# A two-layer model's routing rounds, spread over 128 partitions and summed by TensorE

## The reference

```python
def coor_descent(s, k):                     # s: 8 x 512 scores, EPS = 1
    logk = jnp.log(k)                       # k = 256 * 9/8 = 288
    def body(_, ab):
        a, b = ab
        a = EPS * (logk - logsumexp((s + b) / EPS, axis=-1, keepdims=True))
        b = -relu(s + a)
        return (a, b)
    a, b = fori_loop(0, 50, body, (zeros, -s))
    return exp((s + a + b) / EPS)
sel_scores, sel_idx = top_k(scores, 256)
```

## Time and profile before

| | |
|---|---|
| median of 3 runs | 1802.65 us (1799.55 to 1802.8) |
| the profiled execution | 1800.32 us, span of its instructions 1798.6 us |
| mean granted TensorE clock | 0.973 |
| PE / DVE / ACT / POOL busy, share of the span | 91% / 83% / 74% / 75% |
| layer 1 | 571.6 to 1798.6 us |

### The profile page before, as it was taken

One profiled execution on the slowest core, in us unless ns is written; L12 is line 12 of the kernel. 1 busy time (PEld: TensorE's weight loads), 2 busy tenths in 40 slices (PEclk: granted clock), 3 DMA queues, 4 the chain that ended last, 5 costly groups with the idle time before them and its releaser, 6 DMA issues.

```text
span 1798.6 us, 44374 instructions
## 1 busy us (share of the span) xinstructions
PE 1635.7 (91%) x13580; PEld 1007.8 (56%) x13580; DVE 1496.9 (83%) x2798; ACT 1334.3 (74%) x3261; POOL 1354.5 (75%) x1114
## 2 busy tenths in 40 slices
PE   6999899899884868799999999999999989999988
PEld 4676686685662444455456456456546445645645
DVE  6837848668465999989989989989989988988997
ACT  4756657666652777968978988887896897797765
POOL 2807807718644068999899999899998999989995
PEclk9989999999996989999999999999999999999999
DMA  9446445645466644465364546347345446355430
GB/s 279 147 127 144 132 136 142 167 152 120 142 167 167 171 132 108 126 158 136 115 169 118 143 135 153 114 119 175 114 129 133 104 137 176 95 143 154 110 94 25
DMA packets 164993, 247.65 MB, mean 138 GB/s; under 512 B 30776, under 2 KB 109304, under 8 KB 164760
## 3 DMA queue, kind: packets, MB, share of 16 engines
q1 hardware_dynamic: 152472, 228.02, 45.4%
q0 software_dynamic: 12288, 16.79, 4.6%
HBM read 168.08 MB, written 73.50 MB: 134 GB/s over the span
## 4 chain that ended last, share of the span: by engine, by line
PE 36%; DVE 14%; issue 8%; ACT 8%; POOL 1%; DMA 1%; DVEq 0%; SPq 0%; ACTq 0%; POOLq 0%
PE bank L2323 32%; DVE bank L2846 4%; DVE HB L2846 3%; PE bank L2423 3%; ACT bank L2636 2%; DVE HB L2851 2%; DVE SU L2818 1%; ACT PR L2674 1%; ACT PT L2558 1%; POOL HB L2274 1%; DVE nmax L2877 1%; PE bank L2451 1%; DVE rows L2793 1%; PE bank L2333 1%; DVE nmax L2874 0%
## 5 line engine op out<-in xcount | busy, mean ns | idle before, releaser
L2274 POOL TENSOR_TENSOR HB<-DD,BC 128x512 f32<-128x512 f32 x512 | 641.9, 1284 | 102.4 <-DMA DD<-SU 51.8
L2636 ACT ACTIVATE bank<-DD,A 128x512 f32<-128x512 f32 x512 | 350.3, 694 | 108.8 <-DVE HB L2851 68.7
L2280 POOL TENSOR_TENSOR HB<-HB,BC 128x512 f32<-128x512 f32 x256 | 323.1, 1277 | 49.2 <-DVE HB L2846 48.6
L2846 DVE TENSOR_TENSOR_SCAN bank<-bank,HB 128x512 f32<-128x512 f32 x256 | 311.1, 1215 | 25.8 <-ACT bank L2636 21.6
L2846 DVE TENSOR_TENSOR_SCAN HB<-bank,HB 128x512 f32<-128x512 f32 x256 | 310.3, 1212 | 15.7 <-ACT bank L2636 11.7
L2851 DVE TENSOR_TENSOR HB<-bank,BC 128x512 f32<-128x512 f32 x256 | 175.4, 685 | 15.3 <-DVE bank L2846 0.5
L692 POOL DMA_INDIRECT X<-expert_out_scratch,slot x64 | 110.8, 1731 | 63.9 <-DMA expert_out_scratch<-YS 38.1
L2323 PE MATMUL bank<-HB,fold 128*32 128x512 f32 x1024 | 136.8, 606 | 15.0 <-DVE HB L2851 7.1
L2423 PE MATMUL bank<-ident,PR 128*128 128x128 f32 x768 | 113.6, 279 | 18.1 <-ACT PR L2667 8.5
L2423 PEld LDWEIGHTS bank<-ident,PR 128*128 128x128 f32 x768 | 86.8, 141 | 76.3 <-issue 44.9
L2558 ACT ACTIVATE PT<-bank 128x512 f32<-128x512 f32 x192 | 109.1, 597 | 21.4 <-PE bank L2423 19.7
(11 more groups left out here) (287 smaller groups left out, 3591.9 us busy)
## 6 DMA issues: line engine op xcount, KB each, us to landing
DD<-dd_scratch SPq DMA_DIRECT2D x488, 128.0 KB, 3.5
ROW<-row_scratch SPq DMA_DIRECT2D x64, 256.0 KB
BC<-ssm_scratch SPq DMA_DIRECT2D x128, 128.0 KB, 4.1
dd_scratch<-SU SPq DMA_DIRECT2D x16, 1024.0 KB, 6.0
US<-us_scratch SPq DMA_DIRECT2D x32, 512.0 KB, 4.6
us_scratch<-SU SPq DMA_DIRECT2D x15, 1024.0 KB, 6.1
XL<-sorted_scratch SPq DMA_DIRECT2D x92, 128.0 KB, 2.4
expert_out_scratch<-YS SPq DMA_DIRECT2D x92, 128.0 KB, 1.8
```

The source lines that it names most:

```text
L2274: done(pool.tensor_tensor(HB[:, c % HR], du, bc, ALU.mult), "dbu")
L2280: done(pool.tensor_tensor(h, h, bc, ALU.mult), "cg")
L2636: done(act.activation(PD[n % 2][:], delta, ACT.Exp, scale=A[:, k:k + 1]), "dA")
L2846: done(dve.tensor_tensor_scan(h if n % 2 else dA, dA, h, 0.0, ALU.mult, ALU.add), "scan")
```

## The change

The rounds work on all 128 partitions. `spread_es` holds the 8 x 512 values as 128 x 32, 16 partitions to a batch; it has a second load from HBM and a second exponential. `part` is then a partial sum of 32 values on each partition. A new PE step `rs` after each of the 49 `rt` multiplies it with `blocks`, 128 x 128, which has ones where two partitions belong to one batch, so that every partition receives its batch's sum, in column 0 of bank `PY`. The next `rt` reads its limit there. The last sum is made for 8 partitions only. `blocks` lies in the memory of `YR` and is made by POOL in `constants`, three instructions more. `fold` of the first group waits also for `kr` and `keys`, which read the same bank.

```diff
-        es, rows, part = sb("es", [T]), sb("rows", [T]), sb("part", [2])
-        first, kinv = sb("first", [1]), sb("kinv", [1])
+        es, rows, part = sb("es", [T]), sb("rows", [T]), sb("part", [1])
+        first, kinv, spread_es, small = sb("first", [1]), sb("kinv", [1]), sb("spread_es", [T // 16]), sb("small", [T // 16])
+        blocks = YR[:, 0, 0:P]
...
-            ("s_in", [(es[0:B], scr["s"][:].rearrange("b p t -> b (p t)"))]),
+            ("s_in", [(spread_es[:], scr["s"][:].rearrange("b p t -> (b p t)").rearrange("(q j) -> q j", q=P)),
+                      (es[0:B], scr["s"][:].rearrange("b p t -> b (p t)"))]),
...
+                    own.now(pool.memset(blocks, 1.0))
+                    for base, step, channel in ((0, -16, 1), (15, 16, -1)):
+                        own.now(pool.affine_select(out=blocks.rearrange("p (g r) -> p g r", r=16),
+                                                   in_=blocks.rearrange("p (g r) -> p g r", r=16),
+                                                   compare_op=ALU.is_ge, fill=0.0, base=base,
+                                                   pattern=[[step, B], [0, 16]], channel_multiplier=channel))
...
+                def sum_blocks(i):
+                    after(pe, "rt", 0, i)
+                    if i == 0:
+                        pe.wait_ge(s["consts"], BLOCKS)
+                    if i < ROUTE_ITERS - 2:
+                        q = mm(PY[:, 0:1], blocks, part[:])
+                    else:
+                        q = mm(PY[0:B, 0:1], blocks.rearrange("p (g r) -> p g r", r=16)[:, :, 0], part[:])
+                    done(q, "rs")
...
                     if g == 0:
                         pe.wait_ge(s["consts"], CONSTS)
+                        after(pe, "kr", 0, 0)
+                        after(pe, "keys", 0, 0)
...
-                    act.wait_ge(over["s_in"], 16)
+                    act.wait_ge(over["s_in"], 32)
+                    act.activation(spread_es[:], spread_es[:], ACT.Exp)
                     done(act.activation(es[0:B], es[0:B], ACT.Exp), "es")
...
                 def limit(i):
                     if i:
-                        after(dve, "rt", 0, i - 1)
-                        return part[0:B, (i - 1) % 2:(i - 1) % 2 + 1]
+                        after(dve, "rs", 0, i - 1)
+                        return PY[:, 0:1]
...
                     r = limit(i)
-                    done(dve.scalar_tensor_tensor(out=rows[0:B], in0=es[0:B], scalar=r,
-                                                  in1=kinv[0:B].broadcast_to([B, T]), op0=ALU.min, op1=ALU.mult,
-                                                  accum_out=part[0:B, i % 2:i % 2 + 1]), "rt")
+                    done(dve.scalar_tensor_tensor(out=small[:], in0=spread_es[:], scalar=r,
+                                                  in1=kinv[:].broadcast_to([P, T // 16]), op0=ALU.min, op1=ALU.mult,
+                                                  accum_out=part[:]), "rt")
```

More of the change, by code:

```diff
@@ L1555 @@
[L1555 to L1560, removed]
[10 rows of a table removed]
-    "silu": [[67, 71, 69, 68], [513], [1097], [1760], [2360], [3014], [3651], [4274]],
@@ L1572 @@
[L1572 to L1579, removed]
@@ L1884 @@
[L1884 to L1888 removed]
+    "xt": [[0, 1], [391, 432], [951, 1012], [1643, 1645], [2288, 2291], [2899, 2900], [3528, 3531], [4125, 4122]],
@@ new lines @@
+    "xrt": [[50, 65], [671, 681], [1318, 1356], [1990, 2001], [2651, 2653], [3233, 3269], [3903, 3904], [4464,
+        4580]],
+    "xrtc": [[51, 66], [672, 682], [1319, 1364], [2002, 2003], [2652, 2656], [3234, 3270], [3905, 3906], [4465,
+        4581]],
+    "gam": [[64, 55, 54, 185, 184, 149]],
+    "proj": [[73, 136, 167, 158, 81, 145, 148, 182, 267, 174, 244, 315, 317, 388, 345, 343, 390, 444, 413, 428, 591,
[10 rows of a table added]
+    "silu": [[82, 87, 86, 83], [560], [1158], [1786], [2423], [3069], [3700], [4323]],
@@ new lines @@
+    "dtb": [[94]],
+    "abs": [[95, 96, 97, 98], [636, 612, 613, 656], [1220, 1214, 1215, 1265], [1882, 1863, 1881, 1895], [2517, 2507,
+        2515, 2518], [3160, 3139, 3156, 3161], [3801, 3782, 3783, 3816], [4410, 4401, 4441, 4411]],
+    "projc": [[104, 137, 168, 197, 193, 146, 194, 196, 268, 195, 254, 353, 357, 398, 356, 344, 399, 449, 414, 429,
[10 rows of a table added]
+    "us_st": [[105, 225], [562], [1175], [1862], [2506], [3128], [3778], [4324]],
+    "ssm": [[107], [561], [1168], [1803], [2424], [3089], [3710], [4366]],
@@ new lines @@
+    "relu": [[125, 126, 134, 135], [751, 750, 642, 704], [1269, 1250, 1231, 1232], [1977, 1848, 1845, 1847], [2637,
+        2636, 2477, 2478], [3272, 3271, 3120, 3127], [3932, 3931, 3813, 3814], [4526, 4483, 4435, 4436]],
+    "gsilu": [[128]],
+    "sln": [[144, 159], [703], [1323], [1950], [2576], [3211], [3886], [4511]],
+    "del": [[156, 279], [752, 705], [1367, 1324], [2020, 1951], [2638, 2577], [3277, 3219], [3933, 3887], [4548,
+        4525]],
+    "du": [[157, 339], [767, 766], [1408, 1377], [2031, 2000], [2678, 2578], [3278, 3221], [3934, 3910], [4566,
+        4565]],
@@ new lines @@
+    "dd_ld": [[160, 162, 164, 163, 203, 166, 400, 405, 534, 538, 539, 540, 655, 659, 661, 667], [824, 823, 850, 849,
[7 rows of a table added]
+    "dbu": [[161, 176, 183, 199, 175, 200, 305, 269, 329, 311, 310, 328, 365, 366, 392, 382, 389, 386, 406, 407,
[28 rows of a table added]
+    "asc": [[186]],
[29 rows of a table added]
+    "scan": [[190, 245, 248, 252, 287, 277, 306, 307, 354, 351, 360, 359, 375, 374, 403, 383, 418, 395, 425, 424,
[28 rows of a table added]
+    "score": [[201, 209, 259, 296, 441, 494, 554, 606, 650, 688, 714, 746], [829, 844, 982, 1039, 1155, 1233, 1244,
[5 rows of a table added]
+    "max": [[202, 205, 223, 226, 266, 260, 301, 316, 460, 442, 495, 496, 557, 563, 625, 607, 673, 651, 693, 689,
[10 rows of a table added]
@@ new lines @@
+    "turnc": [[264, 253, 289, 265, 303, 293, 415, 381, 486, 504, 572, 601, 618, 635, 668, 645, 732, 725, 726, 742,
[39 rows of a table added]
+    "recx": [[257, 304, 313, 347, 662, 779], [892, 901, 1100, 1195, 1348, 1440], [1560, 1589, 1660, 1711, 1963,
+        2051], [2147, 2228, 2312, 2467, 2605, 2704], [2826, 2902, 2942, 3048, 3228, 3326], [3432, 3525, 3590, 3667,
+        3867, 3988], [4104, 4192, 4265, 4393, 4533, 4578], [4697, 4791, 4923, 4932, 5077, 5165]],
+    "kr": [[258]],
+    "keys": [[262]],
+    "fold": [[276, 364, 385, 416, 452, 479, 544, 559, 602, 630, 654, 694, 744, 782, 835, 868], [908, 938, 976, 1017,
[7 rows of a table added]
@@ new lines @@
+    "kst": [[282]],
+    "value": [[284, 348, 371, 528, 617, 643, 683, 684, 762, 783, 785, 847], [965, 1019, 1146, 1218, 1292, 1327,
[5 rows of a table added]
+    "spread": [[290, 312, 346, 524, 690, 806], [893, 966, 1122, 1196, 1349, 1451], [1577, 1631, 1708, 1835, 1971,
+        2063], [2193, 2255, 2343, 2494, 2615, 2746], [2827, 2941, 3047, 3140, 3250, 3360], [3522, 3560, 3643, 3727,
+        3898, 4004], [4165, 4206, 4357, 4394, 4542, 4673], [4781, 4820, 4931, 4962, 5121, 5168]],
+    "spreadc": [[291, 314, 350, 527, 691, 807], [911, 968, 1128, 1222, 1354, 1466], [1584, 1657, 1709, 1836, 1976,
+        2064], [2197, 2263, 2345, 2495, 2621, 2747], [2891, 2945, 3051, 3155, 3257, 3391], [3524, 3561, 3644, 3747,
+        3899, 4010], [4182, 4207, 4358, 4404, 4543, 4688], [4785, 4851, 4963, 4979, 5123, 5175]],
@@ new lines @@
+    "norm": [[295, 349, 410, 529, 692, 848], [967, 1021, 1147, 1225, 1357, 1488], [1656, 1690, 1780, 1879, 1980,
+        2101], [2259, 2302, 2412, 2523, 2622, 2770], [2932, 2983, 3061, 3165, 3259, 3409], [3526, 3575, 3696, 3797,
+        3900, 4043], [4199, 4248, 4384, 4428, 4547, 4690], [4786, 4902, 4964, 5002, 5131, 5182]],
+    "widen": [[302, 367, 434, 553, 712, 881], [1011, 1054, 1160, 1262, 1370, 1509], [1669, 1697, 1795, 1914, 1985,
+        2123], [2290, 2315, 2413, 2533, 2642, 2788], [2949, 2984, 3063, 3177, 3275, 3421], [3537, 3579, 3704, 3811,
+        3927, 4044], [4247, 4267, 4427, 4456, 4560, 4705], [4845, 4921, 5001, 5033, 5132, 5183]],
@@ new lines @@
+    "ranks": [[338], [777], [1423], [2103], [2685], [3329], [3973], [4609]],
+    "dd_st": [[340], [788], [1409], [2032], [2681], [3279], [3955], [4574]],
+    "sel": [[363, 362, 341, 342], [818, 890, 891, 830], [1434, 1536, 1537, 1435], [2113, 2115, 2117, 2114], [2727,
+        2794, 2803, 2732], [3330, 3371, 3438, 3331], [3974, 3996, 4014, 3975], [4610, 4683, 4622, 4629]],
+    "xg": [[369], [910], [1554], [2202], [2868], [3480], [4063], [4796]],
+    "h_load": [[], [370], [936], [1558], [2238], [2876], [3481], [4102]],
@@ L1889 @@
+    "out": [[1023, 1006, 1022, 1016], [1611, 1605, 1603, 1602], [2272, 2260, 2258, 2195], [2978, 2977, 2976, 2975],
+        [3548, 3547, 3540, 3462], [4262, 4261, 4259, 4249], [4853, 4852, 4770, 4769], [5209, 5212, 5211, 5210]],
+    "tailp": [[], [], [], [], [], [], [], [5188, 5197, 5200, 5202]],
 }
@@ L2058, in layer1 @@
         ]
-        CONSTS = 9
+        CONSTS, BLOCKS = 9, 12
```

(2 more changed lines are left out.)

150 lines of the change are left out of this document (59 added, 91 removed), and 512 rows, old and new, of the table L1_ORDER.

## The result

The changed kernel took 1812.9 us (median of 10 runs, 1808.9 to 1818.3) against 1802.7 for the kernel before on the same chip: a ratio of 1.0057, interval 1.0041 to 1.0073. That is 10 us slower, where 6 were forecast. The profiled execution of the changed kernel took 1814.11 us.

What follows compares the result with a forecast made beforehand. It took DVE to bound layer 1's opening, with rounds a dependent chain. DVE lateness 5, toll 2 and clock 3.5, less 4.5 given back, made +6 us: 1806.3 profiled, 1808.5 us median, range 1791 to 1822.

Steps and rivals of the forecast that it cites:

- the trip: Layer 1's opening: one round from DVE to PE and back, put at 0.8 us, against 0.78 before.
- A first sum: PE's queue: the first sum of each of 22 groups finds its partial ready and costs about 0.25 us.
- the 27 whole trips: PE's queue in the opening: the other 27 sums each cost a whole 0.8 us, 21.6 us in all.
- the 3.6 us put ahead of them: Net extra DVE work before the keys: 5.9 us moved ahead, 2.3 left for later.
- the toll: Opening: rounds slowed beside POOL's products; 2 us taken, between 0.4 and 5.4.
- growth with length: Opening: if slowing beside POOL scales with a round's length, 0.06 us per round, 0.4 in all.
- the clock, +3.5: Opening, PE: one clock drop slows two projections to 3.45 us each, +3.5 us; bounds nothing to +31.
- Rival (d): PE's clock stays at 1.2 GHz through the rounds, +15 to +31 us on PE, 1820 to 1835; chance 0.10.
- so I give back 60% of DVE's: -4.5: From 670 to 760 us, DVE's 7.35 us idle gaps absorb 4.5 us of the 10.5 us lateness.
- I count 0 for it, with 4 us either way: Reordered table behind the opening: equal work up to each scan, so 0 us, with 4 either way.
- (b): DVE's freed time in the opening counts: 5 to 11 us faster, 1792 to 1798; chance 0.28.
- (c): Idle gaps absorb the opening's lateness: within 0.2%, 1799 to 1806 us; chance 0.20.

Runs made afterwards that it cites:

- rounds22: The changed kernel with 27 of its 49 rounds left out, only the first of each group kept; ratio to the kernel before 1.0018.
- woven: The changed kernel with PE's 49 sums placed inside and between projections, `dtb` and `ssm`; ratio to the kernel before 1.0053.
- one_input: The changed kernel with each round a tensor_scalar reading `spread_es` alone, 1/288 moved into `blocks`; ratio to the kernel before 1.0074.
- before_psum: The kernel before with its rounds' constant 1/288 read from PSUM instead of SBUF; ratio to the kernel before 0.9934.
- new_open_old_rest: The changed kernel's rounds and opening order up to scan 16 of batch 0, then the old order; ratio to the kernel before 1.0041.
- old_order: The changed kernel's rounds in the old table, each sum right behind its round; ratio to the kernel before 1.0198.
- new_mid: The kernel before with the new order only from scan 16 of batch 0 to the first scan of batch 3; ratio 1.0049.
- order_only: The kernel before's rounds, without PE sums, in the whole new table; ratio to the kernel before 1.0038.
- old_open_new_rest: The kernel before's rounds and opening up to scan 16 of batch 0, then the new order; ratio to the kernel before 1.0029.
- before_rounds22: The kernel before with 27 of its 49 rounds left out; ratio to the kernel before 0.9986.
- new_late: The kernel before with the new order only from the first scan of batch 3 on; ratio to the kernel before 0.9980.

## Why the prediction was right, and where it was not

**Right: a round gets no shorter.** Forecast 0.80 us for the trip, measured 0.74 (0.94 at 1.2 GHz). A first sum was put at 0.25 of the queue; it lasts 0.28, but the next product starts 0.14 behind it. A projection with its sum was put at 1.72 + 0.25 = 1.97 and took 1.94.

**Right: PE's queue makes the keys late.** The first sum was due at 582.3 and came at 583.93 - 2.4 = 581.5, counted as before; the keys at about 651 and came at 654.77 - 2.4 = 652.4; `xg` at 675 and came at 675.0. That it is PE's queue is shown by rounds22 (27 sums less put `xg` on time) and by woven (keys 8 us sooner, `xg` 1.0). The price of the 27 whole trips, 21.6 us, was right as a length and not as a cost: without them the keys came only 7.0 sooner. DVE was put at 5 us late; its ranks came 98.3 - 90.1 = 8.2 late. The keys were 10.6 late in the layer and not 9, and of the 3.6 us put ahead of them only 2.4 came back by the ranks, 0.9 of the missing 1.2 because `keys` met POOL and took 1.33 us instead of 0.47.

**Right in size: the toll.** Four rounds beside POOL took 0.91, 0.80, 1.02 and 0.53 instead of 0.26, together 2.2 us; 2 was taken. The mechanism is turns, not growth with length. The Trainium skill, SBUF — State Buffer, section Who interferes with whom, says that a VectorE instruction with two SBUF inputs and a GpSimd one that reads SBUF shut each other out, and that one with a single input, outside the modes that use two ports, does not; one_input (no round above 0.251) and before_psum agree. Its 5 us did not come about, because only four rounds met a product.

**Right for another reason: the clock, +3.5.** The drop near 595 came (0.50 from 594.3 to 601.1). But before had the same one, so it cost nothing anew. The second drop had the other effect: 13.6 us at 0.50 instead of 17.0, but now with a projection in it, 3.76 us for 1.72, and that is 2 of the 3.5. What the other 1.5 should be, no run shows. Rival (d) fell.

**Wrong: "so I give back 60% of DVE's: -4.5".** The sum up to there, 10.5, is what the opening alone costs in the layer (new_open_old_rest, 11.3 late at scan 8, 10.4 at the end). Of this 0.9 was given back. old_order says it more plainly: 34.7 late at scan 8, 37.8 at the end. The timed runs alone would not settle it: 7.4 us (3.6 to 11.4) for new_open_old_rest holds the forecast 6 too. DVE's idle time from 670 to 760 was 90 - 83.03 = 6.97 us, against 7.35: the gaps were not eaten, which fits that what they end with came as late as DVE itself. before_psum says the same from the other side: 5.0 us of lead at scan 8 became 3.8 by the end.

**Wrong: "I count 0 for it, with 4 us either way".** The rest of the table alone costs 10.8 us in the layer, 5.2 (1.8 to 8.7) by its ratio, 7.9 of them between scan 16 of batch 0 and batch 3 (6.3 in the changed kernel, 10.4 in new_mid). Counting each engine's work up to each scan could not see it. The work was the same; the folds and decays came later, and POOL and DVE waited for them. That the table costs is shown by three kernels without a sum in them; that it costs more than the 4 us I gave as a bound is shown by new_mid (5.8 to 11.9), while the intervals of order_only and old_open_new_rest reach below 4.

**Why the total is near the forecast all the same.** In part by luck. The forecast had 6 us for the opening and 0 for the table behind it. By the ratios the opening alone is worth 7.4 us and the rest of the table alone 5.2, together 12.6, where the whole change took 10.3 (7.4 to 13.2): by them the two losses may simply add, and the total is above the forecast because a second loss was left out. By the layers they do not add: 10.4 and 10.8 make 11.4. There, from scan 16 of batch 0 to batch 3 the new table cost 14.9 - 8.6 = 6.3 us behind the late opening and 8.0 - 0.1 = 7.9 behind the early one; from there to the last scan it gave 2.4 back in the one and lost 3.8 in the other. With one execution behind each length, and two of the same queues up to 3.8 us apart, it is not shown that one loss hides the other. The direction would have been right by either half alone.

**The rivals.** (b), that DVE's relief counts, fell twice: the keys were late, and 21 us taken from DVE at no price at all (before_rounds22) made the layer 5.1 us shorter and the ratio 0.9986 (0.9969 to 1.0003). (c), absorption, fell with the result itself and with new_open_old_rest, whose ratio begins at 1.0020.

## What to carry to other kernels

A chain of small dependent steps is bound by the trip, not by the engine's pass: moving part of it to another engine pays only if both queues have something to do in the trip, and the freed engine's time was the limit (here 21 us of it were worth 5 at most). Before such a rewrite, look at what slows the chain's instructions: one operand moved to PSUM took the clash with POOL away and gave 0.9934 alone, the best of all kernels here, though only 0.9978 together with new_late's table, which alone gave 0.9980. And a table that is ordered anew is a change by itself: run it with the old steps before its effect is put down to anything else, and compare scan by scan, since equal work up to each point says nothing of who waits at it.

## What the runs showed of the hardware that was not expected

- The two passes that cut the keys (`kr` and `keys`) read one SBUF operand and collect no sum. Beside POOL they took 1.86 and 1.16 us in before_psum, against 0.72 for `kr` in the changed kernel (at 652.90, begun ahead of POOL's product at 653.13) and 0.47 for `keys` in the one before, while rounds with one SBUF operand and an accumulator kept their 0.735. So one SBUF input is not enough to be left alone: it is the form too. The Trainium skill's page SBUF — State Buffer, in the same section, names `tensor_scalar`, but not the form that writes out its accumulator, among those that can take the shared ports; these rows agree.
- A one-column float32 sum over 128x128 weights lasts 0.28 us behind a product and 0.38 after a wait, 0.59 at 1.2 GHz. The way DVE, PE, DVE took 0.74 us, of which 0.26 is DVE's pass.
- The granted clock fell where PE did sums with gaps between them (0.57 over 690 to 710 us in woven, PE busy 71%), and the projection behind them took 3.62 us instead of 1.72.
